# Routing part of the last mixture's rows inside the second attention's loop, and norming the mixture stage's first rows one stage early

## The reference

```python
x = x + dilated_cross_attention(layernorm(x), ctx)     # first attention
x = x + mixture_block(layernorm(x))                    # attention and MLP with gated experts
x = x + causal_cross_attention(layernorm(x), ctx)      # second attention: 16 heads of 16 channels
x = x + routed_experts(layernorm(x))
...
# routed_experts, 8 experts of 256x256
logits  = x @ router_w.T + router_b
weights = max(softmax(logits))
top1    = argmax(softmax(logits))
out     = (x @ expert_w[top1].T + expert_b[top1]) * weights
```

## Time and profile before

| | |
|---|---|
| runs of the kernel | 2970.12, 2971.11, 2972.57 us (median 2971.11) |
| the profiled execution: its time | 2972.52 us |
| its span, first to last instruction | 2970.6 us, granted clock 0.983 |
| PE busy | 2804.2 us, 94% |
| DVE, ACT, POOL busy | 2250.2, 1862.2, 1576.7 us |
| second attention, 548 us | PE busy 524.2, DVE 466.6, ACT 479.8, POOL 327.5 |
| routed experts, 217.6 us | PE busy 164.5, DVE 109.8, ACT 99.6, POOL 136.5 |

### The profile page before, as it was taken

The page is one execution under the profiler, slowest core; times in us unless marked ns, Lnnn a source line. Parts: engine busy times, 40 slices in busy tenths (PEclk is TensorE's granted clock), DMA queues, the critical chain, the costliest instruction groups (busy, mean ns, idle before and its releaser), DMA issues. The chain is left out here.

```text
span 2970.6 us, 85324 instructions
## 1 busy us (share of the span) xinstructions
PE 2804.2 (94%) x26904; PEld 2563.3 (86%) x26904; DVE 2250.2 (76%) x6197; ACT 1862.2 (63%) x6938; POOL 1576.7 (53%) x1816
## 2 busy tenths in 40 slices
PE   6999999799999999998899999999989999999858
PEld 5888888689999999997899999999988888887446
DVE  6988888877777777776877777777768888888635
ACT  5889898755555555555444444444458988988535
POOL 3666666466666666665322222222216666665566
PEclk9999999999999999999999999999999999999979
DMA  6000000010000000000100000000010000000254
GB/s 226 20 16 15 18 14 15 2 63 11 11 11 11 11 11 11 11 11 13 37 11 11 13 12 11 11 11 11 5 47 16 18 14 18 14 18 2 100 158 146
DMA packets 56375, 87.46 MB, mean 29 GB/s; under 512 B 6958, under 2 KB 42799, under 8 KB 55472
## 3 DMA queue, kind: packets, MB, share of 16 engines
q1 hardware_dynamic: 48848, 66.97, 7.2%
q0 software_dynamic: 6528, 16.92, 1.6%
q10 hardware_dynamic: 864, 1.84, 0.2%
HBM read 58.28 MB, written 28.48 MB: 29 GB/s over the span
## 5 line engine op out<-in xcount | busy, mean ns | idle before, releaser
L564 ACT ACTIVATE L_probs<-bank,L_neg_max 128x128 f32<-128x128 f32 x2048 | 716.7, 402 | 124.4 <-DVE L_neg_max L638 123.8
L564 ACT ACTIVATION_READ_ACCUMULATOR L_probs<-bank,L_neg_max 128x1 f32 x2048 | 497.4, 243 | 0.0
L644 DVE COPY L_probsT<-bank 128x512 f32<-128x512 f32 x512 | 341.8, 687 | 111.8 <-PE bank L447 110.2
L1745 ACT ACTIVATE M_inter<-bank 128x512 f32<-128x512 f32 x256 | 153.2, 598 | 391.5 <-PE bank L69 391.5
L67 PE MATMUL bank<-W_hi,M_nT_hi 128*128 128x384 f32 (+1 forms) x1024 | 370.4, 362 | 8.1 <-DVE M_qkv L1347 4.2
L638 DVE TENSOR_REDUCE L_neg_max<-bank 128x4 f32<-128x512 f32 x512 | 327.7, 682 | 29.8 <-PE bank L437 29.7
L69 PE MATMUL bank<-W_lo,M_nT_hi 128*128 128x384 f32 (+1 forms) x1024 | 347.3, 339 | 0.0
L68 PE MATMUL bank<-W_hi,M_nT_lo 128*128 128x384 f32 (+1 forms) x1024 | 346.8, 339 | 0.0
L1807 DVE TENSOR_TENSOR M_inter_lo<-M_inter,M_inter_hi 128x512 fp32r<-128x512 f32 x256 | 186.4, 729 | 175.1 <-ACT M_inter_hi L1746 167.3
L447 PE MATMUL bank<-constants,L_probs 128*128 128x128 f32 x2048 | 304.1, 281 | 12.8 <-ACT L_probs L564 10.7
L67 PE MATMUL bank<-W_hi,M_inter_hi 128*128 128x256 f32 x1024 | 294.5, 288 | 4.0 <-DVE M_inter_lo L1807 2.1
(11 more groups left out here) (339 smaller groups left out, 9028.5 us busy)
## 6 DMA issues: line engine op xcount, KB each, us to landing
L_ctx_in<-in_ctx SPq DMA_DIRECT2D x64, 256.0 KB, 2.6
M_tile<-M_sorted SPq DMA_DIRECT2D x72, 130.0 KB, 2.2
x_all<-in_x SPq DMA_DIRECT2D x8, 1024.0 KB, 10.4
raw_weights<-in_weights SPq DMA_DIRECT2D x2, 4096.0 KB, 15.0
hs<-M_hs SPq DMA_DIRECT2D x64, 128.0 KB, 1.7
M_hs<-hs SPq DMA_DIRECT2D x32, 256.0 KB, 2.6
raw_weights<-in_weights SPq DMA_DIRECT2D x1, 2048.0 KB, 8.1
M_sorted<-M_fill SPq DMA_DIRECT2D x12, 130.0 KB
```

The source lines that it names most:

```text
L564: last = act.activation(probs[:, k % UNITS, i, :], score_bank[u][:, i, :], ACT.Exp, bias=neg_max[:, u, i:i + 1], scale=-1.0, accum_out=sum ...
L644: dve.tensor_copy(probsT[:, k % UNITS], pT_ps[k % UNITS]).then_inc(pT_ready, 1)
L1745: act.activation(inter[:, e % 2], up_bank[e % 2], ACT.Gelu).then_inc(M.inter_ready, 1)
```

## The change

1. **Second attention.** Seven of the eight groups (56 sequences) are routed here. In each of pairs 3 to 30 the rows of the pair three before (`LAG`) are copied by POOL (`keep_rows`), turned by PE after the first half's scores (`turn_x`), evicted by ACT (`keep_x`) and multiplied with the router by PE in the second half (`dot_router`, now with the rows as weights, so that nothing is turned back); DVE keeps the result. The steps of `choose`, `address` and `weigh` for a group of 8 sequences are spread over the four pairs behind it, by d = p - 4g - 3, each at the end of a half, ahead of the next `row_max`. POOL does the group's root (`group_root`) ahead of `split_q` at d = 4 and sends two sequences per pair from d = 7 (the last sent group four per pair): 48 sequences in the loop. ACT, DVE, POOL and SP have all 32 pairs written out; PE loops over four pairs per turn. Both `busy` calls go; `places` of the seventh group stands in their place, and its further steps follow on DVE.
2. **Routed experts.** Only the eighth group is routed and only 16 sequences are sent; the bias is split ahead of it and all `rest_w` follow `table`.
3. **Mixture attention and MLP.** SP loads the first two sequences' rows again near the end of the mixture attention, DVE norms, scales and shifts them there behind the last statistics, and the MLP stage starts with turning them.

```diff
+GROUP = 4
+GS = 2 * GROUP
+LAG = 3
...
+def turn_x(pe, S, X, rows, bank):
+    out = bank.rearrange("p (k t) -> p k t", k=KT)
+    for k in range(KT):
+        for s in range(2):
+            last = pe.transpose(out[:, k, s * P:(s + 1) * P], rows[:, s, k * P:(k + 1) * P], S.ident[:])
+    last.then_inc(X.xT_made, 1)
...
+def keep_x(act, X, r, b, bank):
+    act.wait_ge(X.xT_made, r + 1)
+    wait(act, X.dots_made, r - 1)
+    act.activation(X.xT[:, b], bank.rearrange("p (k t) -> p k t", k=KT), ACT.Copy).then_inc(X.xT_kept, 1)
...
+def dot_router(pe, R, X, r, b, out):
+    pe.wait_ge(X.xT_kept, r + 1)
+    for s in range(2):
+        for k in range(KT):
+            last = pe.matmul(out[:, s, :], X.xT[:, b, k, s * P:(s + 1) * P], R.raw[:, k, :], start=k == 0, stop=k == KT - 1)
+    last.then_inc(X.dots_made, 1)
...
+def group_root(pool, S, X, g):
+    at = slice(GS * g, GS * (g + 1))
+    pool.wait_ge(X.norm_step, VAR_STEPS * (g + 1))
+    pool.tensor_tensor(S.rows[:, at, C + 1], S.var[:, at], S.minus_half[:, 0:1].broadcast_to([P, GS]), ALU.pow
+                       ).then_inc(X.rooted, 1)
...
+def send_row(pool, S, X, s, signal):
+    g = s // GS
+    pool.wait_ge(X.slots_ready, g + 1)
+    pool.wait_ge(X.weighed, 2 * g + 2)
+    pool.indirect_dma_start(X.sorted_rows, bass.IndirectOffsetOnAxis(X.slots[:, s:s + 1], 0), S.rows[:, s, :], None
+                            ).then_inc(signal, 16)
...
+    def logits(self, g, dots):
+        dve, S, R, X = self.dve, self.S, self.R, self.X
+        at = slice(GS * g, GS * (g + 1))
+        over = lambda t: t.unsqueeze(1).broadcast_to([P, GS, E])
+        by_token = lambda t: t.unsqueeze(2).broadcast_to([P, GS, E])
+        then = self.chained(X.logit_step, 5 * g)
+        dve.wait_ge(X.rooted, g + 1)
+        wait(dve, X.exp_done, g)
+        then(dve.scalar_tensor_tensor(S.rows[:, at, C], S.mean[:, at], -1.0, S.rows[:, at, C + 1], ALU.mult, ALU.mult))
+        then(dve.tensor_tensor(X.offset[:], over(X.column_sums[:]), by_token(S.rows[:, at, C]), ALU.mult))
+        then(dve.tensor_tensor(X.offset[:], X.offset[:], over(R.bias[:]), ALU.add))
+        then(dve.tensor_tensor(X.logit[:], dots, by_token(S.rows[:, at, C + 1]), ALU.mult))
+        then(dve.tensor_tensor(X.logit[:], X.logit[:], X.offset[:], ALU.add))
...
+        routed = lambda p: not first and not (isinstance(p, int) and (p < LAG or p >= NP - GROUP + LAG))
...
+        def groups(p):
+            return [(g, p - GROUP * g - LAG) for g in range(LAST + 1)] if not first else []
...
+            if not first:
+                for p in range(NP):
+                    step(p, p % 2)
+                return
...
                         score(p, b, s)
+                        if s == 0 and routed(p):
+                            turn_rows(p, b)
                             project_k(p + 2, b)
+                        if s == 1 and routed(p):
+                            route(p, b, j, g)
...
+                        if s == 0 and routed(p):
+                            pe.wait_ge(X.xT_kept, p - LAG + 1)
+                        if s == 1 and routed(p):
+                            routed_rows_read(p, j, g)
                         for half in range(2):
                             if s == 0 and more(p, 1):
...
+                    pairs(pe, step)
+                else:
+                    pe.wait_ge(X.sums_kept, 1)
+                    groups_of_pairs(pe, step)
...
                 if not first:
-                    busy(pe, S, 6, 14)
+                    places(pe, S, X, LAST, last_place_ps)
                 for s in range(2):
                     project_o(NP - 1, s)
-                if not first:
-                    busy(pe, S, 6, 10)
...
+                def keep_routed(p):
+                    r = p - LAG
+                    dve.wait_ge(X.dots_made, r + 1)
+                    for g, d in groups(p):
+                        if d == 5:
+                            choice.place(g, place_ps)
+                    at = 2 * (r % GROUP)
+                    dve.tensor_copy(X.dots[:, at:at + 2, :], dots_ps).then_inc(X.dots_kept, 1)
+                def choice_steps(p, s):
+                    for g, d in groups(p):
+                        if (d, s) == (3, 0):
+                            choice.mean(g)
+                        if (d, s) == (3, 1):
+                            choice.var(g)
+                        if (d, s) == (4, 0):
+                            dve.wait_ge(X.dots_kept, GROUP * (g + 1))
+                            choice.logits(g, X.dots[:])
+                        if (d, s) == (4, 1):
+                            choice.best(g)
+                        if (d, s) == (5, 0):
+                            choice.choose(g)
+                        if (d, s) == (5, 1):
+                            choice.address(g)
+                        if (d, s) == (6, 0):
+                            choice.add_up(g)
+                        if (d, s) == (6, 1):
+                            choice.weigh(g)
...
                             row_max(p, UNITS * s + u)
+                        if s == 1 and routed(p):
+                            keep_routed(p)
                         keep_p(p, UNITS * s)
...
+                def keep_rows(r):
+                    pool.wait_ge(x_done, r + 1)
+                    wait(pool, X.xT_made, r)
+                    pool.tensor_tensor(X.rows[:], S.x[:, 2 * r:2 * r + 2, :], S.one.unsqueeze(2).broadcast_to([P, 2, C]), ALU.mult
+                                       ).then_inc(X.rows_kept, 1)
...
                     spread(p, 0)
+                    for g, d in groups(p):
+                        if d == 4:
+                            group_root(pool, S, X, g)
                     if more(p, 1):
                         split_q(p + 1)
+                    send_rows(p, 0)
+                    if routed(p + 1):
+                        keep_rows(p + 1 - LAG)
                     normalize(p, 0)
                     spread(p, 1)
+                    send_rows(p, 1)
...
+                def send_rows(p, half):
+                    for g, d in groups(p):
+                        if g < LAST - 1 and 7 <= d < 11:
+                            send_row(pool, S, X, GS * g + 2 * (d - 7) + half, X.scattered)
...
+                    sp.dma_start(normed[:], hs_dram[0:2].rearrange("s t c -> t s c")).then_inc(next_loaded_rows, 16)
...
+                    if is_(s, NS - 2):
+                        load_first_rows()
...
+                def norm_next():
+                    dve.wait_ge(next_loaded_rows, 16)
+                    for n in range(2):
+                        dve.tensor_scalar(normed[:, n, :], normed[:, n, :], S.mean[:, n:n + 1], S.rstd[:, n:n + 1],
+                                          ALU.subtract, ALU.mult).then_inc(next_normed, 1)
+                def affine_next():
+                    w, b = (t[:].unsqueeze(1).broadcast_to([P, 2, C]) for t in next_ln)
+                    dve.wait_ge(next_normed, 2)
+                    dve.tensor_tensor(normed[:], normed[:], w, ALU.mult).then_inc(next_scaled, 1)
+                    dve.wait_ge(next_scaled, 1)
+                    dve.tensor_tensor(normed[:], normed[:], b, ALU.add).then_inc(next_scaled, 1)
+                    dve.wait_ge(next_scaled, 2)
...
-                describe_late()
-                for g in range(NG):
-                    choose(g)
-                    weigh(g)
-                    address(g)
-                    if g == 0:
-                        split_bias()
-                    for e in range(E):
-                        if e // 2 == g - 1:
-                            rest_w(e)
+                choice = Choice(dve, S, R, X, END)
+                choice.mean(END)
+                choice.var(END)
+                dve.memset(sums[:], 0.0).then_inc(M.set, 1)
...
+                split_bias()
+                dve.wait_ge(X.dots_made, NP)
+                choice.logits(END, dots_ps)
+                choice.best(END)
+                choice.choose(END)
+                choice.place(END, place_ps)
+                choice.address(END)
+                choice.weigh(END)
+                choice.add_up(END)
                 table()
+                for e in range(E):
+                    rest_w(e)
```

472 lines of the change are left out of this document (244 added, 228 removed).

## The result

The changed kernel takes 3021.11 us (median of 4 runs, 3019.48 to 3024.76) against 2971.07 for the kernel before: ratio 1.0165, 95% interval 1.0154 to 1.0177, so 50 us slower. The prediction was 2977 with a range to 3000.

The account below looks back on a forecast made before the run. PE was taken to set the pace of the second attention's loop, ACT and DVE close behind. The terms -4.4 + 0.5 + 44.8 + 35.5 + 1 - 72 = +5.4 us on 2971.1 gave 2977 us, range 2948 to 3000.

Parts of the forecast that it names:

- Start of the mixture MLP and of the second attention: Rows normed ahead start the MLP stage earlier, -4.4 us; fills and column sums on PE at the second attention's start, +0.5.
- PE's own work: Second attention: turnings, router products and a share of `places` add 1.6 us per pair, 28 pairs, +44.8 us.
- the end of 35.0: Lower case for PE's routing work in the second attention: 35.0 us if it also filled PE's idle 0.35 per pair.
- The group's steps: Second attention, DVE: small steps ahead of `row_max` delay it, 5.3 us per group, +35.5 us with the last pairs.
- the pair at d = 4: Second attention: `logits` waits for POOL's root, then meets `split_q`; `row_max` at 14.2, pair 20.9 us, +2.9 and 0.3 for clock.
- the 6.7 us: Second attention: assumed time from a late `row_max` to the next scores, chosen between 6.36 and 7.45 us.
- What those steps meet: Second attention: DVE's steps wait for `split_q` on POOL, two waits of 1.05 us at d = 4; POOL's copy and sends cost nothing.
- The branch: PE's loop of four pairs in the second attention: branches back may stall for instruction fetch; nothing charged in the forecast.
- the second rival: Second attention: late halves cost as in the first attention, 53 us for 35.5, plus 2 for instruction loading: 2997 us, chance 0.20.
- The end of the attention: Without `busy`, the last output projection may run at half clock, +1 us.
- The last stage: Routed experts: first store comes 38.4 us after the stage's start against 110.3, -72 us.
- the forecast case: Whole kernel: the summed terms hold, 2977 us, with its own range 2965 to 2988, chance 0.50.

Follow-up runs that it names:

- the last version: Changed kernel with PE's loop written out, POOL's root and copy behind `add_bo`, DVE's steps mid second halves, router products kept ahead of them except d = 4: 2933.88 us, ratio 0.9866.

## Why the prediction was wrong

The shares, each from two kernels that differ in that alone (the steps' move takes PE's `places` and ACT's exponentials of the group with it), on the loop's ruler; they sum to the +117.3. They hold for this order: with POOL's part taken away first, it is 26.5 and the steps 28.7, and the branch, taken away last, is 29.4.

| cause | from | us |
|---|---|---|
| PE's branch over four pairs | changed kernel to loop written out | 23.4 |
| DVE's steps ahead of `row_max` | from there to steps in second halves | 32.6 |
| POOL's root and copy at that place | from there to both behind `add_bo` | 22.6 |
| products kept behind the steps | to the last version | 6.2 |
| what is left: PE's floor (28), 0.2 to 0.3 more at d = 4 and 6, the first pair | last version to before | 32.5 |

Point by point:

- *Start of the mixture MLP and of the second attention*: -4.4 + 0.5 = -3.9 predicted, -4.5 in the traces; alone the first measured -2.5. Right within the noise: the first scores come at 2218.1 to 2219.4 in three profiles without the routing, one of them with the rows normed ahead, and at 2212.2 to 2217.8 in the changed kernel and its variants, which are all alike up to there.
- *PE's own work*: 1.6 per pair predicted, 1.0 measured (17.45 against 16.43), 28 instead of 44.8. In pair 4 the four turnings and the eight products take 0.49 and 0.88 from their start to the next row's, near the forecast 0.57 and 0.92. But other rows get shorter, the score products (L629) from 2.19 to 2.01, the turning of the normed rows (L568) from 0.69 to 0.60, some of the projections a little, while the wait at the pair's head stays (0.44 for 0.35). So there was room on a PE that looked 97% full, beyond even the end of 35.0 that the prediction named and didn't take. What makes those rows shorter was not followed.
- *The group's steps*: 35.5 predicted, 61.4 measured (32.6 + 22.6 + 6.2). This is the first step that failed: the price of the steps, and above all the pair at d = 4. With PE's loop written out the pairs at d = 3, 5 and 6 take 19.2, 18.3 and 18.4, where the prediction had 19.2, 18.3 and 18.6 (only pairs 6, 8 and 14 are longer, 21.3, 19.8 and 20.5). That is luck in part: the floor under them was 0.6 too high, `row_max` 0.2 to 0.5 too early (it stands at 13.0, 11.8 and 12.3), and the 6.7 us from there to the next scores too many (6.2 to 6.5). At d = 4 the prediction had `row_max` at 14.2 and the pair at 20.9; they are 16.2 (pair 7: 15.1) and 23.2 to 24.4, and 25.1 to 25.4 ahead of a branch.
- *What those steps meet*: the meeting with `split_q` was right, and so was its mechanism: rows of 0.95 and 1.01, the lock of the Trainium skill (SBUF — State Buffer, "Who interferes with whom"). But only two waits were charged, as in the earlier trace rows. In the changed kernel the send and the copy of rows follow `split_q` at once, and at d = 4, where the root has pushed them back, the last step met them: 1.82. In pair 6, where no send stands between, the copy met the third step: 0.96, and the pair took 21.0. The change's own copy had been costed at nothing, by counting POOL's idle time, and not asked what it would meet on DVE. And where PE stood for long, 6.7 us were too few: pair 6 shows 7.5, pair 7 8.0 and the d = 4 pairs ahead of a branch 8.8 to 9.0, with the granted clock at its lower level in part of them (pair 11: from 2435.96 to 2442.79). The prediction had 7.45 in hand and chose the other end because "PE there was not at half clock"; it was, from 174.79 to 178.21.
- *The branch*: nothing in the forecast, 2 us in the second rival, 23.4 measured, and 29.4 where nothing covers it. This is the second step that failed. The rule of the Trainium skill (Runtime: NRT & Kernel Launch, "Instruction fetch mechanics"), that a taken branch outside of the window stops the engine for a fetch, came true for the long loop: stops and instruction packets stand together at each of its branches back. For the short one the traces decide against two pages as the window: the Trainium skill counts 256 instructions to one, and the kernel before branches back over 929 PE records (5368 and 5370 in 23.1 pairs) with neither stop nor packet. The changed kernel has 1964 in a turn (245 and 246 per pair). The prediction put the branch aside by rows of the short loop, and these don't bear on a long one.
- *The end of the attention*: +1 predicted; from the last pair's scores to the last stage's first row 22.8 for 18.5 before, +4.3. With DVE's steps moved it is 20.4, so some 2 of it are late steps of pair 31; the warm matmuls give back 0.7 (19.7).
- *The last stage*: -72 predicted, -69.6 measured (110.3 to 40.7 us to the first store), and 1.1 more behind it.
- *The range*: its upper end of 2988 for the forecast case doesn't follow from its own terms. Half of the second rival's surplus is 8.8, and 0.5 at the end of each of the groups' 24 second halves is 12, which comes to 2998. The measured time lies above both.

Of the rivals the second (2997) was the nearest: late pairs at the first attention's price and a lower clock. Its 2 us for the loading of instructions came from no row. The truth lies 24 above it: 21.4 more for the branch and 8.4 more for the steps, 16.8 less for PE's own work, and the other 11 in small pieces at the attention's two ends and in the last stage.

## What to carry to other kernels

Work moved into a loop that is full on one engine is priced by its place, not by its length: the same steps cost 61 us ahead of the row maximum and next to nothing in the middle of the second halves, where the neighbouring engine was idle. A short DVE instruction may cost one whole instruction of POOL, so list what POOL issues in the next microseconds, the change's own additions first. When a loop's body grows, check its head in the trace for idle time put down to issue, and the DMA records for instruction packets at each turn.

## What was not expected of the hardware

- The branch back over some 1960 PE records stops PE twice, for 3.45 us ahead of the first instruction and for 2.36 three matmuls later, each beside a 16 KB instruction packet; over 929 records it shows no stop and no packet. Where between the two the limit lies was not measured.
- Instructions with a single input in SBUF wait for POOL as well: `mean_steps`' third step, a TENSOR_SCALAR of 128x8, took 0.96, and the CAST of `add_up` 0.97, each beside a POOL instruction, and 0.17 otherwise.
- Near the end of a wait of 3.57 us in PE the granted clock fell to its lower level, for 6.8 us (from 2435.96), and eight turnings took 1.86 us instead of 1.04. In the next pair it fell again for 6.8 us (from 2446.20), during the stop at the branch. Each brings the mean of a pair to 0.86.
- The meeting with DVE holds up POOL as well: a send takes 4.88 us beside eight `rest_w` and 0.96 otherwise.
- At two of the times of measuring the last stage of every kernel was 24 to 40 us longer, with waits of about 2 us on DVE and POOL and no other stage touched. The ratio of 0.983 would have passed for a gain of 1.7%; with the 40 and 24 us taken off, an estimate, it is 1.1%.
